# Finer semaphore waits, transposed maxima in a maximum bank, the first norm in halves, and a new order of side steps in a window-attention and ternary-FFN layer

## What is computed

```python
qkv  = x @ Wqkv + bqkv                      # 16 heads of 16 features
# blocks of 128 queries; each sees its own block of keys, the one before, the one after, |kpos-qpos| <= 128
attn = softmax(scores / 16 + mask)
x = layernorm(x + (attn @ v) @ Wout + bout)
Wq = clip(round(W / (mean|W| + 1e-5)), -1, 1)           # both FFN weights become ternary
x = layernorm(x + relu(x @ Wq1.T + b1) @ Wq2.T + b2)
```

## Time and profile before

| | |
|---|---|
| time, median of 3 | 1196.81 us (1191.0 to 1200.02) |
| the profiled execution | 1195.88 us, its span 1194.1 us |
| busy share of the span: PE, DVE, ACT, POOL | 88%, 72%, 51%, 44% |
| mean granted clock of PE | 0.934 |

### The profile page before, as it was taken

One profiled execution on the slowest core, in us unless ns is written; L12 is line 12 of the kernel. 1 busy time (PEld: TensorE's weight loads), 2 busy tenths in 40 slices (PEclk: granted clock), 3 DMA queues, 4 the chain that ended last, 5 costly groups with the idle time before them and its releaser, 6 DMA issues.

```text
span 1194.1 us, 28091 instructions
## 1 busy us (share of the span) xinstructions
PE 1055.2 (88%) x8132; PEld 772.8 (65%) x8132; DVE 859.5 (72%) x2934; ACT 613.2 (51%) x1258; POOL 521.0 (44%) x824
## 2 busy tenths in 40 slices
PE   4788899998989899898989999898989989897966
PEld 3454676766667576666767676666757666675755
DVE  3875787778787777778777777878777777877233
ACT  4154564555455564655456465545556465554421
POOL 2124353544545444453535354454544446354330
PEclk9576899999999999999999999999999999897879
DMA  5835244434244443444244443425444344422000
GB/s 167 108 51 94 29 82 81 68 68 71 55 77 65 80 71 75 59 81 67 48 80 80 81 65 68 71 53 78 65 80 71 75 59 71 61 50 55 11 9 18
DMA packets 56924, 80.51 MB, mean 67 GB/s; under 512 B 7729, under 2 KB 27697, under 8 KB 56882
## 3 DMA queue, kind: packets, MB, share of 16 engines
q1 hardware_dynamic: 56882, 80.00, 39.8%
HBM read 20.19 MB, written 8.39 MB: 24 GB/s over the span
## 4 chain that ended last, share of the span: by engine, by line
PE 74%; DVE 12%; issue 7%; POOL 2%; ACT 2%; DMA 1%; DVEq 1%; SPq 0%; POOLq 0%; ACTq 0%
PE shared L498 18%; PE st_a L473 12%; PE shared L517 12%; PE shared L596 10%; PE shared L609 9%; PE st_b L473 4%; DVE mx L830 4%; PE shared L592 3%; PE shared L578 2%; DVE rmax L830 2%; DVE x L922 2%; POOL ln_rstd L1036 1%; PE mx L489 1%; DVE oT_lo L877 1%; PE shared L557 1%
## 5 line engine op out<-in xcount | busy, mean ns | idle before, releaser
L830 DVE CUSTOM_DVE_ANT_0 mx<-mx,band 128x384 f32<-128x384 f32 (+1 forms) x1024 | 480.7, 514 | 197.3 <-PE mx L489 194.2
L684 ACT ACTIVATE probs<-st_a 128x384 f32<-128x384 f32 (+1 forms) x384 | 201.9, 526 | 367.8 <-PE st_a L473 362.2
L489 PE MATMUL mx<-k_stack,q_stack 48*128 48x384 f32 (+1 forms) x1024 | 272.6, 368 | 7.0 <-DMA k_stack<-qk_lo 4.0
L997 POOL TENSOR_SCALAR_AFFINE_SELECT probs<-probs 128x512 f32<-128x512 f32 (+1 forms) x256 | 129.7, 530 | 318.6 <-ACT probs L684 318.6
L684 ACT ACTIVATE probs<-st_b 128x384 f32<-128x384 f32 (+1 forms) x384 | 200.8, 523 | 0.2 <-PE st_b L473 0.2
L473 PE MATMUL st_a<-q_stack,k_stack 50*128 50x384 f32 (+1 forms) x512 | 185.1, 403 | 3.1 <-ACT probs L684 2.4
L489 PEld LDWEIGHTS mx<-k_stack,q_stack 48*128 48x128 f32 x1024 | 164.7, 199 | 12.4 <-DVE rmax L830 7.8
L517 PE MATMUL shared<-probs,v_aug 128*32 128x384 f32 (+1 forms) x2048 | 161.6, 446 | 0.8 <-DVE x L922 0.8
L473 PEld LDWEIGHTS st_a<-q_stack,k_stack 50*128 50x128 f32 x512 | 89.7, 196 | 101.6 <-issue 63.0
L830 DVE DVE_READ_ACCUMULATOR2_ANT rmax<- 128x1 f32 x1024 | 143.7, 140 | 0.0
L596 PE MATMUL shared<-x1T_hi,w1q 128*128 128x256 f32 x512 | 143.5, 296 | 0.0
(11 more groups left out here) (107 smaller groups left out, 1962.0 us busy)
## 6 DMA issues: line engine op xcount, KB each, us to landing
q_stack<-qk_hi SPq DMA_DIRECT2D x128, 128.0 KB, 4.3
k_stack<-qk_hi SPq DMA_DIRECT2D x128, 128.0 KB, 5.3
x_raw<-in_xT SPq DMA_DIRECT2D x16, 512.0 KB, 5.0
q_stack<-qk_lo SPq DMA_DIRECT2D x64, 128.0 KB, 3.9
k_stack<-qk_lo SPq DMA_DIRECT2D x64, 128.0 KB, 5.4
y<-in_x SPq DMA_DIRECT2D x16, 512.0 KB, 6.0
out<-x SPq DMA_DIRECT2D x32, 256.0 KB, 2.1
probs<-in_w2T SPq DMA_DIRECT2D x1, 1024.0 KB, 10.6
```

The costliest lines, as they stand in the source:

```text
L489: mm = pe.matmul(PMX[i % N_MAX][:, col:col + n], SQ[rows, hd, W * m:W * m + W], SK[rows, hd, k0:k0 + n], start=True, stop=True)
L684: act.activation(PR[:, v % 2, g // 2, lo:lo + n], PST[i % 2][:, 0:n], ACT.Exp, scale=SCALE) \
L830: mx = dve.tensor_tensor_reduce(ps, ps, band, 1.0, -3e38, ALU.add, ALU.max, RMAX[:, g, m:m + 1])
L997: pool.affine_select(out=pr_before, in_=pr_before, compare_op=ALU.is_ge, fill=0.0, base=0, pattern=[[0, n], [1, W]], channel_multiplier=-1)
```

## The change

- `SIDE`: stage 0 does `ot,0` right after `nmt` and takes `ln1,0` and `ln1,1` in front of `op,1`. Stage 1 begins with `ln1,2` and `ln1,3`, and does `qk,3` before `ut` and not after `x1t,1`.
- `nmt` no longer takes a shared bank. The transpose goes into the bank of the maximum unit that comes next (`NMT_AT`, unit 2 in all four stages, hence bank `mx2`), and that unit waits on PE until ACT has written the transpose out (`s_nmt`). The turn of the shared banks shifts with it.
- `ln1` on POOL is done in two halves, for tiles 0, 1 and for tiles 2, 3.
- Waits are split: `op` waits for its two halves of `oT` one by one, `ot` for the quads that it reads, `x1t` tile by tile, `f1` and `f2` for halves and pairs at the matmul that reads them.
- ACT does its part of `nmt` and `pvb` before the exps woven into that step, not after.

```diff
SIDE = [
-    [("qk", 0), "nmt", "pva", "pvb", ("vp", 0), "ut", ("vp", 1), ("ot", 0), ("ot", 1), ("qk", 1), ("op", 0),
-     ("op", 1)],
-    [("ln1", 0), ("ln1", 1), ("ln1", 2), ("qk", 2), "nmt", ("ln1", 3), "pva", "pvb", ("x1", 0), ("x1", 1),
-     ("x1", 2), ("x1", 3), "ut", ("x1t", 0), ("x1t", 1), ("qk", 3), ("f1", 0, 0)],
+    [("qk", 0), "nmt", ("ot", 0), "pva", "pvb", ("vp", 0), "ut", ("vp", 1), ("ot", 1), ("qk", 1), ("op", 0), ("ln1", 0),
+     ("ln1", 1), ("op", 1)],
+    [("ln1", 2), ("ln1", 3), ("qk", 2), "nmt", "pva", "pvb", ("x1", 0), ("x1", 1), ("x1", 2), ("x1", 3), ("qk", 3),
+     "ut", ("x1t", 0), ("x1t", 1), ("f1", 0, 0)],
...
-USES_BANK = {"pva", "ut", "qk", "ot", "op", "vp", "x1t", "f1", "f2", "nmt"}
+USES_BANK = {"pva", "ut", "qk", "ot", "op", "vp", "x1t", "f1", "f2"}
...
+def units_before(v, step, kind):
...
+    return sum(k == kind for woven in WOVEN[v][:SIDE[v].index(step)] for _, k, _ in woven)
...
+NMT_AT = [units_before(v, "nmt", "max") for v in range(QUADS)]
+assert max(NMT_AT) < UNITS
...
         s_rs1 = sem("ln1_rstd_done")
+        s_neg = sem("ln1_neg_mean_done")
         s_nmr = sem("neg_mean_rstd")
-        s_x1 = sem("x1_done")
+        s_x1a = sem("x1_done_by_act")
+        s_x1d = sem("x1_done_by_dve")
...
                         else:
-                            sp.wait_ge(s_x1, 4 * b)
+                            sp.wait_ge(s_x1a, 2 * b)
+                            sp.wait_ge(s_x1d, 2 * b)
...
                     pe.wait_ge(s_mxr, 12 * (4 * r + v) + i - N_MAX + 1)
+                if i == NMT_AT[(v + 2) % 4] and not (first and v == 0):
+                    pe.wait_ge(s_nmt, 4 * r + v)
...
-            def split3(ps, lhs, rhs, passed):
+            def split3(ps, lhs, rhs, passed, chunk=None):
...
                     passed()
+                    if chunk is not None and n % 3 == 0:
+                        chunk(kc)
...
                 elif name == "nmt":
-                    pe.wait_ge(s_nm, 4 * r + vq + 1)
-                    pe.transpose(G[:, 0:W], NMW[:, :], IDN[:, :]) \
-                        .then_inc(s_nmtf, 1)
-                    reader[n] = (s_nmt, 4, vq + 1, dr)
+                    q, i = 4 * r + vq, NMT_AT[v]
+                    pe.wait_ge(s_nm, q + 1)
+                    if i >= N_MAX and max_quad(v, at) is not None:
+                        pe.wait_ge(s_mxr, 12 * (q + 1) + i - N_MAX + 1)
+                    pe.transpose(PMX[i % N_MAX][:, 0:W], NMW[:, :], IDN[:, :]).then_inc(s_nmtf, 1)
...
                     i = step[1]
-                    pe.wait_ge(s_on, 4 * r + 4)
+                    pe.wait_ge(s_on, 4 * r + 2 * i + 2)
...
                     i = step[1]
-                    pe.wait_ge(s_oth, 2 * r + 2)
-                    pe.wait_ge(s_otl, 2 * r + 2)
...
+                    def oT_half(kc):
+                        pe.wait_ge(s_oth, 2 * r + kc + 1)
+                        pe.wait_ge(s_otl, 2 * r + kc + 1)
...
                                     lambda a, kc: OT[a][:, kc, P * t:P * t + P],
-                                    lambda z, kc: WOUT[z][:, kc, :], passed)
+                                    lambda z, kc: WOUT[z][:, kc, :], passed, oT_half if t == 0 else None)
...
                     i = step[1]
-                    pe.wait_ge(s_x1, 4 * r + 4)
...
                         passed()
+                        if i == 0:
+                            pe.wait_ge((s_x1a, s_x1d)[t % 2], 2 * r + 1 + t // 2)
...
                     hf, p = step[1], step[2]
-                    pe.wait_ge(s_x1h, 2 * r + 2)
-                    pe.wait_ge(s_x1l, 2 * r + 2)
...
                         for kc in range(KC):
+                            if hf == 0 and p == 0 and k == 0:
+                                pe.wait_ge(s_x1h, 2 * r + kc + 1)
+                                pe.wait_ge(s_x1l, 2 * r + kc + 1)
...
                     hf = step[1]
-                    pe.wait_ge(s_hh, 8 * r + 4 * hf + 4)
-                    pe.wait_ge(s_hl, 8 * r + 4 * hf + 4)
...
                         for f in range(FC):
+                            if t == 0 and f % 2 == 0:
+                                pe.wait_ge(s_hh, 8 * r + 4 * hf + f // 2 + 1)
+                                pe.wait_ge(s_hl, 8 * r + 4 * hf + f // 2 + 1)
...
                         act.wait_ge(s_nmin[(vq + 2) % 4], 16 * r + (0 if vq < 2 else 16))
-                    act.activation(NMT[:, vq % 2], G[0:8 * NB, 0:W], ACT.Identity).then_inc(s_nmt, 1)
+                    act.activation(NMT[:, vq % 2], PMX[NMT_AT[v] % N_MAX][0:8 * NB, 0:W], ACT.Identity).then_inc(s_nmt, 1)
...
                     t = step[1]
-                    act.wait_ge(s_nmr, 2 * r + 2)
+                    act.wait_ge(s_nmr, 2 * r + t // 2 + 1)
...
                     act.activation(X1[:, t, :], Y[:, t, :], ACT.Identity, bias=NMR1[:, t:t + 1],
-                                   scale=RS1[:, t:t + 1]).then_inc(s_x1, 1)
+                                   scale=RS1[:, t:t + 1]).then_inc(s_x1a, 1)
...
                             other_weights()
+                        row = row_of(v, step, at)
+                        before = name_of(step) in ("nmt", "pvb")
+                        if row is not None and before:
+                            side_work(v, step, b, *row, at)
...
                                 exp(b, v, i, at)
-                        row = row_of(v, step, at)
-                        if row is not None:
+                        if row is not None and not before:
...
                         dve.wait_ge(s_mv2, 4 * r)
-                        dve.wait_ge(s_x1, 4 * r)
+                        dve.wait_ge(s_x1a, 2 * r)
+                        dve.wait_ge(s_x1d, 2 * r)
...
                     dve.bn_stats(ST[:, t, :], Y[:, t, :]).then_inc(s_st1, 1)
-                    for t in {0: (), 3: (2, 3)}.get(t, (t - 1,)):
+                    for t in ((t - 1, t) if t % 2 else ()):
...
                     t = step[1]
-                    dve.wait_ge(s_rs1, r + 1)
+                    dve.wait_ge(s_rs1, 2 * r + t // 2 + 1)
...
                     dve.tensor_scalar(X1[:, t, :], Y[:, t, :], MV1[:, t, 0:1], RS1[:, t:t + 1],
-                                      ALU.subtract, ALU.mult).then_inc(s_x1, 1)
+                                      ALU.subtract, ALU.mult).then_inc(s_x1d, 1)
...
                                        ALU.add).then_inc(s_xrb, 1)
-                elif step == ("ln1", 3):
-                    count = in_register(pool, 4 * r + 4)
+                elif name == "ln1" and step[1] % 2 == 1:
+                    hf = step[1] // 2
+                    two = slice(2 * hf, 2 * hf + 2)
+                    count = in_register(pool, 4 * r + 2 * hf + 2)
...
                     pool.wait_ge(s_mv1, count)
-                    pool.tensor_scalar(VE[:, :], MV1[:, :, 1], 1.0, EPS, ALU.mult, ALU.add).then_inc(s_ve, 1)
-                    pool.wait_ge(s_ve, 3 * r + 1)
-                    pool.tensor_tensor(RS1[:, :], VE[:, :], HALF[:, :], ALU.pow).then_inc(s_rs1, 1)
-                    pool.tensor_scalar(NEG1[:, :], MV1[:, :, 0], -1.0, None, ALU.mult).then_inc(s_nmr, 1)
-                    pool.wait_ge(s_rs1, r + 1)
-                    pool.wait_ge(s_nmr, 2 * r + 1)
-                    pool.tensor_tensor(NMR1[:, :], NEG1[:, :], RS1[:, :], ALU.mult).then_inc(s_nmr, 1)
+                    pool.tensor_scalar(VE[:, two], MV1[:, two, 1], 1.0, EPS, ALU.mult, ALU.add).then_inc(s_ve, 1)
+                    pool.tensor_scalar(NEG1[:, two], MV1[:, two, 0], -1.0, None, ALU.mult).then_inc(s_neg, 1)
+                    pool.wait_ge(s_ve, 4 * r + 1 + hf)
+                    pool.tensor_tensor(RS1[:, two], VE[:, two], HALF[:, two], ALU.pow).then_inc(s_rs1, 1)
+                    count = in_register(pool, 2 * r + hf + 1)
+                    pool.wait_ge(s_const, CONSTANTS)
+                    pool.wait_ge(s_neg, count)
+                    pool.wait_ge(s_rs1, 2 * r + hf + 1)
+                    pool.tensor_tensor(NMR1[:, two], NEG1[:, two], RS1[:, two], ALU.mult).then_inc(s_nmr, 1)
...
                         return
```

More of the change, by code:

```diff
@@ L1051, in side_work @@
                     pool.tensor_scalar(VE[:, two], MV2[:, two, 1], 1.0, EPS, ALU.mult, ALU.add).then_inc(s_ve, 1)
-                    pool.wait_ge(s_ve, 3 * r + 2 + hf)
+                    pool.wait_ge(s_ve, 4 * r + 3 + hf)
                     pool.tensor_tensor(RS2[:, two], VE[:, two], HALF[:, two], ALU.pow).then_inc(s_rs2, 1)
```

## The result

The kernel is slower: 1240.2 us (median of four executions, 1238.0 to 1240.93) against 1193.9 us for the kernel before beside it. The ratio is 1.037, with an interval from 1.033 to 1.041. The profiled span grew from 1194.1 to 1236.3 us, by 42.2 us.

A forecast was written before the change was run, and what follows sets the result against it. PE was taken to bound the kernel (74% of the chain), DVE next. Per full pass -2.1 + 0.5 + 1.7 + 0.5 = +0.6 us, +8 over 14 passes, ends -8.5: -0.5 on 1195.88, so 1196 us, range 1172 to 1218.

The forecast's parts named there:

- Stage 0: First stage of a pass: waits of `qk0` (1.2), `vp0` (0.3) and `op0` (0.6) go, a gain of 2.1 us.
- Stage 1: From `qk2` to `f1,0,0`: two stalls go, four come, 5.35 us for 3.2; the stage takes 16.7 us, 0.5 more.
- the wait of `m2`: Stage 1: unit `m2` waits for ACT to copy the transpose out, and PE loses some 0.75 us.
- that on the exps: Stage 1: `s6` and `s7`, reusing banks, are held by ACT's exps after `u`: 0.5 + 0.2 us.
- that of `x1t1`: Stage 1: `x1t1` waits for the bank of `qk3` to be read out by ACT and DVE: 1.0 us.
- The fourth, at `f1`: End of stage 1: `f1` waits for DVE's low part of `x1t1`, behind `m11` and `neg_max`: some 2.9 us.
- The clock: First `f1` steps, now in stage 2: the same 3.4 us at 1.2 GHz as before, costing 1.7 us.
- the clock stays low twice as long: Rival, first `f1` steps of stage 2: 1.7 us more per pass, +24 us, 1219 us; chance 0.18.
- the statement on transposes: Transposes don't count as PE busy like matmuls; `ut`, `x1t0`, `x1t1` between two gaps would lengthen the time at 1.2 GHz.
- the copies: Stages 2 and 3: maximum units wait for ACT's copy of the transpose, 0.4 and 0.1 us, +0.5 per pass.
- The ends: Outside the full passes: last step 5 us shorter, passes 0 and 15 -1.5 and -2, in all -8.5 us.
- The rival with the waits of `m2`: PE held with `s3`, ACT's exps and `pva`'s mask: twice 1.25 us per pass, +17 us, 1212; chance 0.10.

The follow-up runs named there:

- the version whose clock holds: The kernel after with `qk3` put back behind `x1t1` in stage 1, all else as changed: 1120.02 us, ratio 0.937 to the kernel before.
- the version with the collision put in: The kernel before with POOL's add held back to the end of the maxima of stage 1: 1218.62 us, ratio 1.022.

## Why the prediction was wrong

I forecast 1196 us, and it is 1240, outside the range. The step that failed is the last queue of DVE in stage 1, where `neg_max` stands with 0.6 us, its length before: beside POOL's add it took 2.5 us. A smaller one is the busy time of PE, which grew by more than I had allowed for.

- **Stage 0:** forecast -2.1 us. Its 1.2 us ahead of `qk0` lie before this stage when it is cut at the first matmuls of `qk0` and `qk2`, so -0.9 of it falls here, and -1.4 was measured. Right in kind, half a microsecond better.
- **Stage 1, the step that failed.** I forecast 16.7 us, and it took 19.7. Of the four stalls three are near: the wait of `m2` 0.48 beside the bank (0.75 forecast), that on the exps 0.49 (0.7), that of `x1t1` 0.95 (1.0). The fourth, at `f1`, was to be 2.9 us and is 0.81 + 0.31 + 3.48 = 4.6. Its DVE list has "`neg_max` 0.6 us", the length of before, and its second operation alone took 2.27. From the release of `x1t1` (647.26) to the end of the last `x1T_lo` (653.31 + 0.68) pass 6.73 us; I had 0.8 + 3.9 = 4.7, and the 1.95 us by which that operation grew make it 6.65. The kernel with the add held back shows the same, with a wait on `x1T_lo` of 1.5 us at most where it is 3.6 here. The other 0.8 us of the stage lie ahead of this: `x1t1` was released 12.8 us after the first matmul of `qk2` (647.26 - 634.45), and I had 12.0. The three stalls before it are shorter than forecast, together 1.9 us for 2.45, so it was PE's busy time that was too small in the sum: some 9.6 us, and 10.9 measured. I had taken each duration from the trace of before and had looked at POOL's share of busy time only, not at which POOL instruction would lie beside which DVE instruction once unit 11's mask was ahead of the add. The Trainium skill, "GPSIMD Engine Reference", 1. Specifications, says that GpSimd and VectorE share SBUF interfaces and contend for them, among others where a VectorE instruction has two inputs in SBUF. The trace agrees (0.32 us before, 2.27 us beside the add); that section gives no duration.
- **The clock:** forecast 3.4 us at 1.2 GHz in the first `f1` steps, 1.7 us lost. The stretches of one microsecond of the kernel after:

```profile
650.00:651.00 1.00, 0.48 (x2) 0.30 (x2) 0.97 (x6) 0.00 (x0) 1.00 (x3) 1.00 0.91 186
651.00:652.00 1.00, 0.00 (x0) 0.00 (x0) 0.96 (x2) 0.00 (x0) 1.00 (x2) 0.57 1.05 119
652.00:653.00 1.00, 0.00 (x0) 0.00 (x0) 1.00 (x1) 0.00 (x0) 1.00 (x1) 0.50 1.19 123
...
657.00:658.00 1.00, 1.00 (x6) 0.56 (x5) 0.92 (x4) 0.74 (x2) 0.00 (x0) 0.51 0.48 167
```

  The microsecond from 651 has 0.86 us at 1.2 GHz ((1 - 0.57) / 0.5), and the last of them 0.98, so the clock is low from about 651.15 to 658.0, 6.8 us. PE stands idle in the first 3.0 of them, until 654.13, and is busy in the other 3.8: 1.9 us lost, 0.2 more than forecast. The time at 1.2 GHz is 6.8 us in 12 of the 14 passes. The rival "the clock stays low twice as long" has the duration right and the price wrong: nearly half of it falls into the stall. Why it is twice as long stays open: no run tests on its own the statement on transposes that the prediction took from the Trainium skill.
- **The rest of the pass:** -1.2 at `qk0`, +1.7 for the clock and +0.5 for the copies is +1.0, and +1.0 was measured (33.6 to 34.6 us).
- **The ends:** forecast -8.5, measured -8.4, and that this agrees is in part luck. The forecast had -1.5 in pass 0 and -7 behind the full passes; measured are -3.0 in front, which is no more than the spread there, and -5.4 behind.

In the range I had no case in which a known term grew. The rival with the waits of `m2` had its sign, and not its mechanism. Of the 42 us the collision is 26 (29 by the lengths of the operation). The remaining 1.5% (16 us, 1.1 us a pass) lies in PE's busy time as far as the trace shows. Without what the low clock costs, PE is busy for 61.0 us of a pass before (62.68 - 1.7), for 62.7 after (64.61 - 1.9) and for 62.7 in the version whose clock holds. Beside that growth of 1.7 us `m2` waits idle for 0.48, in all 2.2, where I had 1.25 for lost overlap (0.75 + 0.4 + 0.1). That is 0.9 us a pass. The stage 1 rows show where a part of it is: `s` and `m` of a pair no longer start together (634.77 and 635.01; both at 612.22 before), and from `nmt` to `pva` pass 1.77 us (636.81 to 638.58) for 0.81 before (614.03 to 614.84), only 0.48 of it idle. No run isolates it.

The larger miss lies in how I read the change: I treated `qk3`'s move as one of several equal steps. It is the one that turns a gain of 6% into a loss of 4%, since it takes the 2 us of matmuls between `x1t1` and `f1` away, which covered DVE's last evictions, and so opens the stall at `f1`, during which the clock falls in the pass shown.

## What to carry to other kernels

When an order is changed, lay the new timelines of all engines beside each other, not only the queue of each: a short DVE operation that reads only SBUF took the whole length of the POOL operation that ran beside it here, and a mean over the execution hides it. Look at PE's busy time as well as at its waits: here it grew by more than its idle time. A step that has no dependence on its neighbours was worth most between a product's eviction and its use; take it from there only if something else fills the place. And undo one part at a time before the whole is given up: here all parts but one were a gain of 6% together.

## What was not expected of the hardware

- A DVE operation of 128x16 with two SBUF inputs took 2.25 to 2.32 us beside a POOL `tensor_tensor` of 128x1024 that took 2.34 to 2.39, and 0.17 to 0.32 us otherwise in all passes but the first (once 0.53). Started 0.05 us before the add, it kept its 0.17. The first operation of `neg_max`, a `tensor_scalar` with one SBUF input, took 1.96 to 2.09 us beside the add where it takes 0.17 to 0.62 otherwise, so operations with one SBUF input are held too. What the two have in common that the others have not, as far as these rows go, is that all their inputs are in SBUF. Operations with an input in PSUM kept their length beside the same add (0.69 and 0.75 us).
- The granted clock fell behind two stalls of 1.41 and 1.79 us close together and in the 3.48 us stall of the kernel after. It did not fall in 800 us of the fastest version, whose usual waits are up to half a microsecond. In between, the length of the stalls doesn't decide it alone: one stall of 1.4 us a pass brought 3.4 us at 1.2 GHz in eight passes of 13, stalls of 1.0 and 0.4 us brought 3.4 or 6.8 us in each, and the same pair of 1.41 and 1.79 us brought 3.4 us in a pass of the kernel before and 6.8 us in most passes of the version with the collision put in.
